# Attention B: the products with V and the denominators of a unit in one block behind the fourth score product

## The reference

```
q = (x @ Wq.T).reshape(b, t, 8, 32)
kv_latent = x @ Wkv_down.T
k = (kv_latent @ Wk_up.T).reshape(b, t, 8, 32)
v = (kv_latent @ Wv_up.T).reshape(b, t, 8, 32)
attn = softmax(einsum('bqhd,bkhd->bhqk', q, k) * 32 ** -0.5, axis=-1)
out = einsum('bhqk,bkhd->bqhd', attn, v).reshape(b, t, 256)
return out @ Wo.T
```

## Time and profile before

| | |
|---|---|
| median of three runs | 2250.72 us (2246.54 to 2251.57) |
| profiled execution, its own time | 2249.5 us |
| span of its trace | 2247.7 us |
| mean granted TensorE clock | 0.981 of full speed |
| PE, DVE, ACT, POOL busy | 93%, 85%, 77%, 39% |
| L643, products with V, all units | 0.27 us each, in pipelined rows of 32 |
| L686, exponentials | 0.60 us each, 512 of them |
| L738, row maxima | 1.20 us each, 256 of them |
| L768, pair sums | 1.28 us each, 256 of them |

### The profile page before, as it was taken

How to read it: one execution, slowest core, us unless ns; L and a number is a source line. 1 busy time by engine, 2 the same in 40 slices (tenths; PEclk the granted TensorE clock), 3 DMA queues, 4 the chain that set the end, 5 groups by cost and what they waited for, 6 DMA issues and landing times. The chain is left out here.

```text
span 2247.7 us, 62135 instructions
## 1 busy us (share of the span) xinstructions
PE 2099.7 (93%) x24904; PEld 1428.6 (64%) x24904; DVE 1919.2 (85%) x2618; ACT 1734.8 (77%) x3070; POOL 877.0 (39%) x953
## 2 busy tenths in 40 slices
PE   6799999999999999999999999968779999999877
PEld 4467776777767777777777767754435656566644
DVE  6899999999999999999999999957678788887684
ACT  3789998999989999999999999942357777777532
POOL 4333323333223333333233233233017777777540
PEclk9999999999999999999999999988989999999988
DMA  3799999999999999999999999940141111111001
GB/s 102 119 197 195 195 196 185 195 193 193 193 194 197 194 197 195 191 197 189 198 194 191 194 192 194 197 83 1 35 137 31 30 31 33 34 32 35 9 1 38
DMA packets 1097040, 303.81 MB, mean 135 GB/s; under 512 B 1070256, under 2 KB 1090096, under 8 KB 1096496
## 3 DMA queue, kind: packets, MB, share of 16 engines
q1 hardware_dynamic: 1095888, 299.36, 76.5%
q10 hardware_dynamic: 864, 0.47, 0.1%
HBM read 20.83 MB, written 10.49 MB: 14 GB/s over the span
## 5 line engine op out<-in xcount | busy, mean ns | idle before, releaser
L453 DVE SCALAR_TENSOR_TENSOR a_parts<-a_probs,a_parts 128x1024 f16<-128x1024 f32 x512 | 659.1, 1287 | 79.4 <-ACT a_parts L405 78.7
L364 PE MATMUL a_out_ps<-a_vs,a_pT 128*128 128x128 f16 x4096 | 712.2, 219 | 4.7 <-DMA a_pT<-a_parts 4.6
L366 PE MATMUL a_out_ps<-a_vs,a_pT 128*128 128x128 f16 x4096 | 712.2, 219 | 0.0
L368 PE MATMUL a_out_ps<-a_vs,a_pT 128*128 128x128 f16 x4096 | 712.2, 219 | 0.0
L397 ACT ACTIVATE a_probs<-a_score_ps,a_negmax 128x1024 f32<-128x1024 f32 x512 | 571.4, 1116 | 94.1 <-DVE a_negmax L447 86.6
L447 DVE TENSOR_REDUCE a_negmax<-a_score_ps 128x1 f32<-128x1024 f32 x512 | 622.1, 1215 | 11.0 <-PE a_score_ps L350 7.2
L507 POOL TENSOR_TENSOR a_weighed<-a_own_out,wpost 128x256 f32<-128x256 f32 x256 | 247.1, 965 | 961.3 <-DVE a_parts L453 956.0
L405 ACT ACTIVATE a_parts<-a_probs 128x1024 f16<-128x1024 f32 x512 | 540.3, 1055 | 31.8 <-DMA a_pT<-a_parts 31.0
L364 PEld LDWEIGHTS a_out_ps<-a_vs,a_pT 128*128 128x128 f16 x4096 | 400.8, 98 | 64.8 <-ACT a_own_out L415 4.1
L366 PEld LDWEIGHTS a_out_ps<-a_vs,a_pT 128*128 128x128 f16 x4096 | 400.8, 98 | 59.5
L346 PE MATMUL a_score_ps<-kh,a_qs 128*128 128x512 f16 x1024 | 390.2, 381 | 42.3 <-ACT a_probs L397 34.9
(11 more groups left out here) (221 smaller groups left out, 2262.9 us busy)
## 6 DMA issues: line engine op xcount, KB each, us to landing
a_pT<-a_parts SPq DMA_TRANSPOSE x512, 5.0
b_qs<-q_parts SPq DMA_DIRECT2D x96, 64.0 KB, 1.9
b_ks<-k_parts SPq DMA_DIRECT2D x96, 64.0 KB, 1.9
q_parts<-b_parts SPq DMA_DIRECT2D x32, 128.0 KB, 1.9
k_parts<-b_parts SPq DMA_DIRECT2D x32, 128.0 KB, 1.9
x<-x_dram SPq DMA_DIRECT2D x4, 512.0 KB, 7.6
a_rope<-rope_dram SPq DMA_DIRECT2D x1, 2048.0 KB, 10.4
out_dram<-x SPq DMA_DIRECT2D x4, 512.0 KB, 5.4
```

The costliest lines, as they stand in the source:

```text
L364: pe.matmul(out[:, 0:D], hi, vs[:, b, 0, j, :], start=j == 0, stop=False, skip_group_check=True)
L366: pe.matmul(out[:, 0:D], hi, vs[:, b, 1, j, :], start=False, stop=False, skip_group_check=True)
L368: last = pe.matmul(out[:, 0:D], lo, vs[:, b, 0, j, :], start=False, stop=j == JB - 1, skip_group_check=True)
L453: dve.scalar_tensor_tensor(out=parts[:, T % RING_P, 1, :], in0=probs[:, T % RING_P, :], scalar=PSCALE, in1=parts[:, T % RING_P, 0, :], op0 ...
```

## The change

The two halves of `times_v` become one block that runs behind score 3, that is after `rate` and scores 2, 3 of the next unit. The positions behind scores 1 and behind scores 5 are empty now. Inside the block the waits are finer: the products with V wait for the exponentials two key blocks at a time, and the products with ones for each pair sum. `pv_done` counts once for a unit, no longer once for a half, so ScalarE and GpSimd, which overwrite `probs` and `sums`, now wait for all products of unit u - 2 and not for its first half.

```diff
-            def times_v(u, half):
+            def times_v(u):
 
                 if u < 0:
                     return
-                if half == 0 and u:
+                if u:
                     pe.wait_ge(evicted, u)
-                pe.wait_ge(exp_done, JB * u + 4 * half + 4)
-                for j in range(4 * half, 4 * half + 4):
+                for j in range(JB):
+                    if j % 2 == 0:
+                        pe.wait_ge(exp_done, JB * u + j + 2)
                     for t in range(TILES):
                         pe.matmul(out_ps[t * HDB:(t + 1) * HDB, 0, 0:P], v_all[:, u // 2, j, :],
...
-                pe.wait_ge(added, PAIRS * u + 2 * half + 2)
-                for pair in range(2 * half, 2 * half + 2):
+                for pair in range(PAIRS):
+                    pe.wait_ge(added, PAIRS * u + pair + 1)
                     for t in range(TILES):
...
                 scores(u, 0)
                 scores(u, 1)
-                times_v(u - 1, 0)
                 rate(TILES * (u + 1) + 3)
                 scores(u, 2)
                 scores(u, 3)
+                times_v(u - 1)
                 rate(TILES * (u + 2))
                 scores(u, 4)
                 scores(u, 5)
-                times_v(u - 1, 1)
                 spread_max(u + 1)
                 rate(TILES * (u + 2) + 1)
                 scores(u, 6)
                 scores(u, 7)
-            times_v(units - 1, 0)
-            times_v(units - 1, 1)
+            times_v(units - 1)
...
                 if u >= 2:
-                    act.wait_ge(pv_done, 2 * (u - 2) + j // 4 + 1)
+                    act.wait_ge(pv_done, u - 1)
...
-                act.wait_ge(pv_done, 2 * u + 2)
+                act.wait_ge(pv_done, u + 1)
...
                 if u >= 2:
-                    pool.wait_ge(pv_done, 2 * (u - 2) + pair // 2 + 1)
+                    pool.wait_ge(pv_done, u - 1)
```

## The result

The changed kernel takes 2333.27 us (median of four runs, 2331.84 to 2336.07) against 2251.14 us for the kernel before (four runs): the ratio is 1.0368, with a 95% interval of 1.0355 to 1.0381. It is **82 us slower**; 2342 us was forecast, with a range of 2308 to 2370. The profiled execution took 2336.07 us.

What follows compares the result with a forecast made beforehand. The order of TensorE's work was taken to bound the kernel at 6.84 us a unit; after the change a closed loop of 8.31 us. 63 x 1.47 = 93 us on 2249.5 gave 2342 us, range 2308 to 2370.

Steps and rivals of the forecast that it cites:

- The loop: Attention B: closed chain from score 4 through ScalarE, VectorE and the block to the next score 4, 8.31 us a unit.
- scaled maximum to eviction: ScalarE: step from the scaled maximum to the eviction of the unit before, taken as 0.25 us, bounds 0.12 and 0.29.
- row maximum to the product waiting for it: VectorE to TensorE: from a row maximum to the row-maximum product that needs its bank, 1.28 us.
- the fast block: TensorE: lower bound for the joined products block at the fast matmul pace, 2.55 us against 2.73 taken.
- The spread was to be idle 1.05 us: TensorE: spread waits for ScalarE's scaled maximum behind scores 4, 5; stall 1.21 us a unit, 1.05 seen as idle.
- The wait for the row maximum: TensorE: third row-maximum product of each unit waits for VectorE's row maximum, idle some 0.4 us, some 25 us in all.
- the rival of the falling clock: TensorE's granted clock is cut to half by idle time in every unit: 2600 us and more; chance 3%.
- the finer waits: Block on TensorE: its pair-by-pair waits for exponentials and GpSimd sums cost nothing; about 1.25 us if their cover were gone.
- the coarser releases: ScalarE and GpSimd: waiting for all products of the unit before last costs nothing, being met a whole unit earlier.
- The rival in which only the spread's stall counts: Attention B: VectorE's loop closes earlier, so a unit takes 7.75 us; 57 us slower, 2307 us; chance 6%.
- The faster one: TensorE stays the bound and only the form changes count: 0.26 us a unit shorter, 16 us, 2233 us; chance 4%.
- The forecast's saving of 0.26 us a unit: TensorE: one block instead of two halves saves 0.17 us, and 0.09 for the second entry to the 32-column form.

Runs made afterwards that it cites:

- the link to VectorE cut: Changed kernel with VectorE's reciprocal moved behind row maximum 4u+9 instead of ahead of it, ScalarE unchanged: 2321.25 us, ratio 1.0313.
- all orders: Changed kernel with scaled maximum and eviction ahead of exponentials 4 and 5, reciprocal behind row maximum 4u+9, score 4 directly behind the block: 2257.8 us, ratio 1.0037.

## Why the prediction was right, and where it was off

*The sign and the mechanism.* The argument rested on unit 0, in which score 4 to spread takes 1.65 us with no products between the earlier trace rows. The changed kernel repeats that figure in every unit. The loop was worked out from rows of the kernel before and held term by term:

| term of the loop | forecast | in the changed kernel |
|---|---|---|
| score 4 to exponential 4 | 0.42 | 0.42 |
| exponential 4 to scaled maximum | 0.95 | 0.97 |
| scaled maximum to eviction | 0.25 | 0.09 |
| eviction to reciprocal | 0.40 | 0.41 |
| reciprocal to row maximum | 0.87 | 0.87 |
| row maximum to the product waiting for it | 1.28 | 1.22 |
| product, scores 2 and 3, entry | 0.97 | 0.97 |
| the block | 2.73 | 2.76 |
| row-maximum product before score 4 | 0.44 | 0.44 |
| sum | 8.31 | 8.15 |

*The size.* The forecast was 63 x 1.47 = 93 us; 63 x 1.31 = 82.5 us came, and the medians differ by 82.1. The term that was mis-sized is the step from the scaled maximum to the eviction. It was the one term without a row of its own; I took 0.25 between bounds of 0.12 and 0.29, and the next operation started after 0.09 us, below the lower bound, while the scaled maximum was still shown as running (0.21 us). The row maximum and the product behind it were taken at 1.28 and measured 1.22. That row came from a stretch at a granted clock of 0.50, but the clock is not the reason: the experiment with the reciprocal last has 1.29 at a clock of 1.00. The row maximum of the loop stands right behind the reciprocal, and there it is shown shorter, 1.16 us instead of 1.21 to 1.23:

```profile
1857.13 1.16 DVE L737 TENSOR_REDUCE b_negmax<-b_max_ps 128x1 f32<-128x1024 f32 x1
```

These two terms make 0.22 us; the block, the exponentials and the eviction took 0.06 back. One bound was worked out wrongly: the pace named for the fast block, 0.0247 us a matmul, gives 1.45 + 1.19 = 2.64 us and not 2.55. With it the lower end of the loop would be 8.04 us and 2325 us, still in the stated range.

*The profiled execution.* It was 86.6 us longer than that of the kernel before (2336.07 against 2249.5). The first spread of the stage starts at 1676.84 in it, and at 1673.17 in the kernel before: 3.7 us of the difference lie ahead of the changed code and are not its doing.

*The stalls.* The spread was to be idle 1.05 us: it is. The wait for the row maximum was to be about 0.4 us and is 0.20 as the profile shows it, 0.35 by the distance of the starts; the shorter loop accounts for it. ScalarE's longest wait was to be 2.7 and is 2.64; TensorE busy near 83%, measured 84.8%; clock 1.00, so the rival of the falling clock did not come.

*The costs set to nothing.* The list of waits of the changed kernel has none of a product of the block for ScalarE or GpSimd, and none of ScalarE or GpSimd for the products of the unit before last, so neither the finer waits nor the coarser releases cost anything that shows. The rival in which only the spread's stall counts (2307 us) is refuted by the result, 26 us above it, and by the experiments: with the link to VectorE cut the unit was 7.97 us and not the rival's 7.75, and with the stall taken away it was still 8.06. The faster one (2233 us) is refuted by the result. The forecast's saving of 0.26 us a unit agrees with the 0.24 measured for one change of form and back; the block itself is 0.14 shorter than two halves (2.90 against 2.76) and the entry makes 0.09, 0.23 together.

## What to carry to other kernels

Before work is moved away from a place, ask which other engine used that time. If the trace has a unit in which that work is missing (the first of a pipeline often has), its wait is the price of the move. When afterwards several engines wait in turn and none is full, add up the closed chain and cut it where it is cheapest. Add up the next longest chain too, since it sets what the cut is worth. The largest wait in the list was worth 7 us here when removed alone, and a reciprocal moved behind one row maximum was worth 12, though no large wait pointed to it; both moves on ScalarE together were worth 31. Then look at the engines that the block leaves without work: in the best order that was run, the block of 2.76 us left VectorE idle for 1.59 us, and the unit did not come under 6.84 us. How long a block could be before that happens is not shown by these runs.

## What the runs showed of the hardware beyond that

- On ScalarE a copy started 0.09 us after the start of the small scaling operation ahead of it, which itself is shown 0.21 us long. An exponential started 0.29 us after the start of an eviction shown 0.37 us long (1855.37 to 1855.66, all orders), but the copy of the shift 0.40 us after it. I had expected different operations to follow without overlap; some do overlap.
- A row maximum of 128 x 1024 is shown 1.16 us long right behind the reciprocal and 1.21 to 1.23 us long behind idle time or behind another row maximum, at a granted clock of 1.00.
- One more change of TensorE to the 32-column form and back costs 0.24 us between float16 products of full width, at the granted clock of 1.00, with no work added.
- TensorE at 85% busy, with 1.05 us idle in each 8.15 us, kept a granted clock of 1.00 in every window of 100 us from 1700 to 2200.
